# Moving the decay step and the first window's scores ahead of the value, gate and beta projections, adding waits on weights kept in DRAM, and giving one PSUM eviction to VectorE

## What is computed

```python
q, k, v, gate = (xn @ W.T for W in (Wq, Wk, Wv, Wg))        # xn = layernorm(x)
beta  = sigmoid(xn @ Wb.T)
alpha = exp(-exp(A_log) * softplus(xn @ Wa.T + dt_bias))     # one per head and step
q = q / |q| / sqrt(64);  k = k / |k|
for t in steps:                                              # 16 heads, 64x64 state S
    S = S * alpha[t]
    S = S + k[t] (v[t] - k[t] S) * beta[t]
    y[t] = q[t] S
ctx = rmsnorm(y) * silu(gate)
x = x + layernorm(ctx @ Wo.T + bo)
x = x + layernorm(fp6(layernorm(x)) @ fp6(weight).T + bias)
```

## Time and profile before

| | us |
|---|---|
| timed runs, median of 2 | 6981.89 |
| the profiled execution, its own time | 6975.83 |
| span of its slowest core (core 3) | 6974.3 |
| spans of all cores | 6940.6 to 6974.3 |
| mean granted TensorE clock of the cores | 0.587 to 0.589 of 2.4 GHz |

### The profile page before, as it was taken

The page is one execution under the profiler, slowest core; times in us unless marked ns, Lnnn a source line. Parts: engine busy times, 40 slices in busy tenths (PEclk is TensorE's granted clock), DMA queues, the critical chain, the costliest instruction groups (busy, mean ns, idle before and its releaser), DMA issues.

```text
span 6974.3 us, 73066 instructions; the slowest of 8 cores (6940.6 to 6974.3 us)
## 1 busy us (share of the span) xinstructions
PE 2689.2 (39%) x22136; PEld 1582.8 (23%) x22136; DVE 2770.8 (40%) x6430; ACT 1059.7 (15%) x2275; POOL 679.5 (10%) x1048
## 2 busy tenths in 40 slices
PE   2214144444424334544423424445431515444441
PEld 1101022322301122323311113223210103233320
DVE  2341144444462135444453114444455014444446
ACT  2111111111111111111011211111111211111111
POOL 1100110111000111111000111011000011011000
PEclk9999555555557655555556755555555855555555
DMA  5412021212102121212101112112201212121210
GB/s 88 76 36 63 8 43 34 43 35 39 32 18 70 21 37 32 46 31 42 40 14 53 42 26 45 33 31 47 41 21 36 58 14 46 31 38 40 44 32 21
DMA packets 426947, 269.76 MB, mean 39 GB/s; under 512 B 235380, under 2 KB 413942, under 8 KB 426566
## 3 DMA queue, kind: packets, MB, share of 16 engines
q1 hardware_dynamic: 382790, 212.59, 13.8%
q0 software_dynamic: 43776, 52.49, 5.0%
HBM read 245.93 MB, written 27.44 MB: 39 GB/s over the span
## 4 chain that ended last, share of the span: by engine, by line
DVE 32%; DMA 26%; PE 19%; issue 14%; ACT 6%; DVEq 2%; POOL 0%; SPq 0%; ACTq 0%; POOLq 0%
DMA wrep<-wd 13%; DVE ptm L882 8%; DVE u L886 7%; PE ppr L551 3%; DVE rr L625 3%; PE ptr L891 2%; PE psu L904 2%; DMA wdst<-sc 2%; PE pys L917 2%; DVEq L1202 2%; DVE rr L943 2%; PE pys L845 1%; PE ptr L617 1%; ACT ut L896 1%; DVE st L488 1%
## 5 line engine op out<-in xcount | busy, mean ns | idle before, releaser
L891 PE MATMUL ptr<-idf,u 128*16 128x128 f32 x1024 | 259.1, 407 | 1441.2 <-DVE u L886 1336.8
L808 DVE TENSOR_TENSOR wrep<-wrep,bb 128x2048 f32<-128x2048 f32 x128 | 293.4, 2293 | 1082.7 <-DMA wrep<-wd 1082.7
L882 DVE TENSOR_TENSOR ptm<-wrep,u 128x120 f32<-128x120 f32 (+14 forms) x1920 | 515.1, 268 | 193.7 <-DVE u L886 8.0
L886 DVE TENSOR_TENSOR u<-u,ptm 128x120 f32<-128x120 f32 (+14 forms) x1920 | 451.6, 235 | 206.0 <-DVE ptm L882 8.3
L840 PE MATMUL pkv<-kc,s 64*64 64x16 f32 x4096 | 479.6, 265 | 45.2 <-DVE kc L816 45.2
L840 PEld LDWEIGHTS pkv<-kc,s 64*64 64x64 f32 x4096 | 454.3, 220 | 74.0 <-issue 69.9
L845 PE MATMUL pys<-qc,s 64*64 64x16 f32 x4096 | 460.6, 264 | 21.4 <-ACT ys L924 21.4
L891 PEld LDWEIGHTS ptr<-idf,u 128*16 128x16 f32 x1024 | 100.4, 112 | 1587.9 <-issue 1548.2
L845 PEld LDWEIGHTS pys<-qc,s 64*64 64x64 f32 x4096 | 450.6, 222 | 30.2 <-issue 30.2
L551 PE MATMUL ppr<-lt,wrhs 128*128 128x512 bf16 x1280 | 332.7, 407 | 220.9 <-DMA wrhs<-wtk 30.5
L910 DVE TENSOR_TENSOR s<-s,psu 128x512 f32<-128x512 f32 x128 | 88.1, 688 | 752.2 <-PE psu L904 752.2
(11 more groups left out here) (208 smaller groups left out, 4099.0 us busy)
## 6 DMA issues: line engine op xcount, KB each, us to landing
wrep<-wd SPq DMA_DIRECT2D x256, 512.0 KB, 5.2
sx<-x SPq DMA_DIRECT2D x4, 2048.0 KB, 8.6
ao<-pd SPq DMA_DIRECT2D x32, 256.0 KB, 5.7
out<-sx SPq DMA_DIRECT2D x4, 2048.0 KB, 6.6
wld<-Wf SPq DMA_DIRECT2D x8, 512.0 KB, 5.5
wrhs<-wtq POOLq DMA_DIRECT2D x16, 256.0 KB, 3.8
wrhs<-wtq SPq DMA_DIRECT2D x16, 256.0 KB, 3.1
wrhs<-wtk SPq DMA_DIRECT2D x16, 256.0 KB, 3.1
```

The source lines that it names most:

```text
L808: VE(lambda e, wv=wv, bb3=bb3: e.tensor_tensor(wv, wv, bb3, ALU.mult), [f"wrep{cp}", "bb"], [f"wrep{cp}"], tag="wrepscale")
L882: VE(lambda e, wsl=wsl, ub=ub, ptv=ptv: e.tensor_tensor(ptv, wsl, ub, ALU.mult), ["u", f"wrep{cp}"], ["ptm"], tag="slv_p")
L886: VE(lambda e, usl=usl, ptv=ptv: e.tensor_tensor(usl, usl, ptv, ALU.add), ["u", "ptm"], ["u"], tag="slv_u")
L891: TE(lambda e, hp=hp, hpi=hpi: e.transpose(p_tr[0:16, hpi * 128:(hpi + 1) * 128], s_u[:, hp * C:(hp + 1) * C], s_idf[:]), ["u", "idf", "ptr"],
```

## The change

It has four parts.

- **Weight keys.** Every store of a transposed weight now writes a key of its DRAM tensor ("dwq" to "dwb", "dwo", "dwf", "dwa"), and every load of it reads that key.
- **Decay step first.** In `proj_mm_part` the decay step stands before the five projections.
- **Hook.** After the k projection, `norms_window(sb, 0)` and `scores_and_masks(sb, 0)` are called, and not any more after the whole of `proj_mm_part`. `wrep_load(sb*4, 0)` stays behind it.
- **Eviction.** The second round of the u transposes in each chunk is evicted by VectorE.

```diff
@@ prep_weight (the same in the Wo and Wf rounds, with "dwo" and "dwf")
-                dma("sync", dst, src, ["wtt" + "AB"[hb]], [], tag="wstore")
+                dma("sync", dst, src, ["wtt" + "AB"[hb]], ["dw" + tagn],
+                    tag="wstore")
@@ emit_preamble
         dma("sync", d_wat.rearrange("(fb f) h -> f fb h", f=128),
-            s_wtt[:, 0:128].rearrange("f (fb h) -> f fb h", h=16), ["wttA"], ["wttA"])
-        proj_mm_part(0)
+            s_wtt[:, 0:128].rearrange("f (fb h) -> f fb h", h=16), ["wttA"],
+            ["wttA", "dwa"])
+        proj_mm_part(0, hook=lambda: (norms_window(0, 0),
+                                      scores_and_masks(0, 0)))
@@ proj_mm_part
-    def proj_mm_part(sb):
-        projs = [("q", s_qb, AF.Identity), ("k", s_kb, AF.Identity),
...
+    def proj_mm_part(sb, hook=None):
         src = d_wat.rearrange("(fb f) h -> f fb h", f=128)
         dma("sync", s_wrhs[:, 0:128].rearrange("f (fb h) -> f fb h", h=16), src,
-            ["ws0"], ["ws0"])
+            ["ws0", "dwa"], ["ws0"])
...
+        projs = [("q", s_qb, AF.Identity), ("k", s_kb, AF.Identity),
+                 ("v", s_vb, AF.Identity), ("g", s_gb, AF.Silu),
+                 ("b", s_bb, AF.Sigmoid)]
+        for m, dstt, act in projs:
+            for oc in range(8):
...
+                dma("sync" if par == 0 else "gpsimd",
+                    wsl.rearrange("f (fb o) -> f fb o", o=128), src,
+                    skeys + ["dw" + m], skeys, tag="wstream")
...
+            if m == "k" and hook is not None:
+                hook()
@@ proj_superblock
-        proj_mm_part(sb)
+        proj_mm_part(sb, hook=lambda: (norms_window(sb, 0),
+                                       scores_and_masks(sb, 0)))
@@ chunk_steps
-            SE(lambda e, rnd=rnd: e.copy(
-                s_ut[0:16, rnd * 512:(rnd + 1) * 512], p_tr[0:16, 0:512]),
-               ["ptrw"], ["ptr", "ut"])
+            if rnd == 0:
+                SE(lambda e, rnd=rnd: e.copy(
+                    s_ut[0:16, rnd * 512:(rnd + 1) * 512], p_tr[0:16, 0:512]),
+                   ["ptrw"], ["ptr", "ut"])
+            else:
+                VE(lambda e, rnd=rnd: e.tensor_copy(
+                    s_ut[0:16, rnd * 512:(rnd + 1) * 512], p_tr[0:16, 0:512]),
+                   ["ptrw"], ["ptr", "ut"])
@@ attn_out_batch (the same in ffn_superblock with "dwf")
-                [f"ws{cc}"], [f"ws{cc}"], tag="wostream")
+                [f"ws{cc}", "dwo"], [f"ws{cc}"], tag="wostream")
@@ the window loop
             if wi == 0:
-                norms_window(sb, 0)
-                scores_and_masks(sb, 0)
                 wrep_load(sb * 4, 0)
```

More of the change, by code:

```diff
@@ L431, in prep_weight_alt_iter @@
                 "f (fb o) -> f fb o", o=128)
-            dma("sync", dst, srcs, ["tb" + "AB"[hb]], [], tag="wstore")
+            dma("sync", dst, srcs, ["tb" + "AB"[hb]], ["dwo"], tag="wstore")
     def prep_weight_quant_iter(d_src, d_dst, ob):
@@ L459, in prep_weight_quant_iter @@
                 "f (fb o) -> f fb o", o=128)
-            dma("sync", dst, srcs, ["wtt" + "AB"[hb]], [], tag="wstore")
+            dma("sync", dst, srcs, ["wtt" + "AB"[hb]], ["dwf"], tag="wstore")
     def emit_preamble():
@@ L602, in proj_mm_part @@
                ["pscw"], ["psc", "ppt"])
+        projs = [("q", s_qb, AF.Identity), ("k", s_kb, AF.Identity),
[3 more added lines that the diff above has]
+            for oc in range(8):
+                par = oc % 2
+                wsl = s_wrhs[:, par * 1024:(par + 1) * 1024]
+                src = d_wt[m].rearrange("(fb f) o -> f fb o", f=128)[
+                    :, :, oc * 128:(oc + 1) * 128]
+                skeys = [f"ws{par * 2}", f"ws{par * 2 + 1}"]
+                dma("sync" if par == 0 else "gpsimd",
+                    wsl.rearrange("f (fb o) -> f fb o", o=128), src,
+                    skeys + ["dw" + m], skeys, tag="wstream")
+                for fb in range(8):
+                    sk = f"ws{par * 2 + fb // 4}"
+                    TE(lambda e, fb=fb, wsl=wsl: e.matmul(
+                        p_pr[:], wsl[:, fb * 128:(fb + 1) * 128],
+                        s_lt[:, fb * SBT:(fb + 1) * SBT],
+                        start=(fb == 0), stop=(fb == 7)),
+                       [sk, "lt", "ppr"] if fb == 0 else [sk, "lt"],
+                       ["pprw"] if fb == 7 else [])
+                SE(lambda e, dstt=dstt, oc=oc, act=act: e.activation(
+                    out=dstt[:, oc * SBT:(oc + 1) * SBT], in_=p_pr[:], func=act),
+                   ["pprw"], ["ppr", m + "b"])
+            if m == "k" and hook is not None:
+                hook()
     def win_slice(tile, wi, p0=0, p1=128):
@@ L993, in attn_out_batch @@
                         d_wto[cc * 128:(cc + 1) * 128, oh * 512:(oh + 1) * 512],
-                        [f"ws{par2}"], [f"ws{par2}"], tag="wostream")
+                        [f"ws{par2}", "dwo"], [f"ws{par2}"], tag="wostream")
                 for wi in range(4):
@@ L1017, in ffn_superblock @@
                 d_wtf[fb * 128:(fb + 1) * 128, 0:512],
-                [f"ws{fb}"], [f"ws{fb}"], tag="wfstream")
+                [f"ws{fb}", "dwf"], [f"ws{fb}"], tag="wfstream")
         for wi in range(4):
```

2 lines of the change are left out of this document (1 added, 1 removed).

## The result

| | before | after |
|---|---|---|
| median of the timed runs, us | 6981.71 (6 runs, 6979.05 to 6984.73) | 7054.16 (7 runs, 7046.60 to 7057.03) |
| ratio after/before, 95% interval | | 1.0102 (1.0090 to 1.0115) |
| spans of the cores, profiled execution | 6940.6 to 6974.3 | 7012.6 to 7061.9 |

A forecast was written before the change was run, and what follows sets the result against it. The prediction took queue order, not any full engine, as the bound (no chain line above 13%). Its terms 36 + 2 + 4 + 8 = +50 on 6975.8 gave 7026 us, 8-in-10 range 6975 to 7095.

The forecast's parts named there:

- chain of stores: Preamble, five bf16 weights: each store waits for the previous landing, 3.0 us; 6.1 us a round, +36 us (0 to +59).
- Wa read after its store: `d_wat` is read directly after it is written: one landing of 2.0 us, once, +2 us.
- Wo and Wf loads, semaphore turn: Last Wo and Wf blocks on POOL wait for the load just issued: 0 (at most 16 a superblock, under 0.5 us).
- decay step and hook: Superblock reorder moves the DMA row without covering it: start +2.6, restart +6.2, before first chunk -7.8; +4 us in four.
- eviction: VectorE copy in each chunk takes 685 ns against ScalarE's 576; counted in 68 of 128 chunks, +8 us (0 to +14).
- My own sign of being wrong: Among the profile signs listed as "wrong": a landing below 2.6 us in the chained stores.
- b7 to scaling: Before the first chunk: scaling follows b7 by 6.9 us, against 14.7 from "qkb" to scaling today; -7.8 us a superblock.
- the restart: v, g and b resume after "qkb": load 4.0 us, v0's slow matmuls +1.7, v1's wait +0.5; +6.2 us a superblock.
- Stores wholly hidden: Rival: preamble stores land in 2.6 us or less once chained and cost nothing; 6990 us, chance 0.27.
- Hook overlaps: Rival: 24 projection blocks run under the POOL DMA row, 81 us a superblock, 324 in four; 6702 us, chance 0.03.
- Longest landing: Rival: chained preamble stores take 4.3 us to land, 8.7 us a round, +139; 7129 us, chance 0.05.
- Reorder gains: Rival: superblock reorder gains 24 us instead of costing 4, both "wrep" loads fully hidden; 6998 us, chance 0.1.

The follow-up runs named there:

- Run 4: Kernel after with all its keys, but weight keys left out of the waits when a DMA takes over a semaphore: 7037.57 us, 1.0064.
- run 6: Kernel before plus weight keys, kept out of semaphore takeover; loads wait for all stores of their weight, stores not for one another: 6986.55 us, 1.0004.
- run 5: Kernel before plus weight keys, one key for all stores of a weight, kept out of semaphore takeover: 6991.41 us, 1.0013.
- run 3: Kernel after without the weight keys except "dwa" and with evictions on ScalarE, leaving the reorder alone: 7007.38 us, 1.0020.
- run 1: Kernel before with the weight keys alone, order and evictions unchanged: 7038.88 us, 1.0069.
- run 2: Kernel before with only the second round of u transposes evicted by VectorE: 7007.53 us, 1.0026.
- run 7: Kernel before with both rounds of u transposes evicted by VectorE: 7028.01 us, 1.0058.
- Run 10: Against before: decay step first, hook split, v/g/b loaded by SP, "qkb" later, unchained weight keys, semaphore takeover waiting only for the previous DMA: 6603.20 us, 0.9448.
- plain turns: Kernel before, but a DMA taking over a semaphore waits only for its previous DMA, not that DMA's keys' readers: 6955.61 us, 0.9949.

## Why the prediction was right and where it was wrong

The sign, the size class and the mechanism of the reorder were right. That the sum came near is luck: a term that was some 30 us too large and one of about that size that was missing nearly cancelled.

| term, us | forecast | measured |
|---|---|---|
| chain of stores | +36 (0 to 59) | +5 to +9 in the time, +12 in the cores' mean stage |
| Wa read after its store | +2 | not told apart |
| Wo and Wf loads, semaphore turn | 0 (bound: 16 x 0.5 a superblock) | +27 to +39 |
| decay step and hook | +4 (-24 to +48) | +14 |
| eviction | +8 (0 to 14) | +14 to +18 |
| sum | +50 | +72 |

- **Semaphore turn: the step that failed.** "Each is used three blocks later (4 matmuls each), so I put 0." Two things are wrong in it. The distance of three blocks is no cover: in before the load issued at 3555.84 is used at 3558.30, 2.5 us later, and TensorE already waits 0.41 us for it, so each load is issued about one landing ahead of its use and most of any further wait is exposed (3.9 us from two held loads). And I priced that wait at under 0.5 us, with rows at hand that put the landing of a streamed load at 3.0 to 3.8 us; it was 2.93. The POOL loads come 3.5 us apart (3600.41 and 3603.88) where they came 0.86 us apart. I also had the wait too narrow: "the load just issued" is only one of the loads of that key, and the first of the pair was held 2.5 us by SP's. Run 4 shows the cost (28 us in one stage), run 6 that the keys without it are free.
- **Chain of stores: right mechanism, the landing mis-sized.** Forecast was 3.0 us a landing and 6.1 us a round; measured are medians from 2.3 to 3.4 us by weight and 5.64 us a round on core 3, the stores being the bound only in some weights. Of the two rates that I had weighed, both occur. The 0.06 us behind a landing, for which I gave no row, is what before shows between a "wrep" load's landing (2489.05) and the issue of the next (2489.11). My own sign of being wrong, a landing below 2.6 us in the chained stores, came true: the median is 2.3 or 2.4 us in Wk, Wg and Wb. The Trainium skill (DMA: Bandwidth & Descriptors, Latency and other measured facts) has the fixed cost fall with a lighter load on HBM. Wg's 2.3 us would fit that and Wv's 3.4 would not. No run here shows the load on HBM; this core itself moved more in Wg's stretch (107 GB/s from 203.5 to 243.5 us) than in Wv's (83 GB/s from 152 to 203.5), so its own traffic does not explain the difference, and why the landing differs stays open. The slowest core's time moved less than the stage does: 9 us in run 5 against 16 us on core 3 of after. Whether that is because the longest stage falls on another core than the longest rest, no run separates.
- **Decay step and hook: the overlap right, the clock mis-sized.** In the second superblock of after, core 3: start 14.6 us (2208.77 to 2223.39) against 14.5 forecast; norms to "qkb" 156.2 against 157; b7 to scaling 6.0 against 6.9. Two things failed. The first is the restart, "v0's matmuls are slow again, +1.7": three blocks were slow and not one (+5.0). "qkb" to v0 took 5.8 us and not 4.0, since v0's load, beside the "qkb" load, took 5.1 us to land; v1's load waited the "qkb" load out, as forecast. v0 to b7's end is 83.6 us against 79.7 before (2231.39 to 2311.09), where g2 and g3 had been slow instead. That makes 5.8+3.9 = 9.7 where I had 6.2. The second the sum put at nothing: q0 to k7's end takes 59.3 us against 54.3, because six of these 16 blocks run at 3.57 us where two took 3.5 or more before; less one gap between blocks that falls away, +4.1. The superblock's sum is then 2.7+4.1-0.7+9.7-8.7 = +7, +28 in four; in the cores' mean stage A shows +21, and the time of run 3 +14. So the cost of the reorder is about that of a lower clock in the same matmuls: 30 us more busy time on core 3, 28 in the mean of the cores (325 to 353). How much of that hides behind waits for loads no run separates, and both figures scatter: in runs 1, 2, 5 and 6, whose order is that of before, stage A took 1413 to 1416 us where before took 1407, and these matmuls 329 to 335 us.
- **Eviction: right price, wrong count.** 679 ns against 685 forecast. The 68 chunks (139 us at 2.02 are 69) came from L891's share of the chain, but the chain names one of several waits that end together (my reading; no view shows the others); runs 2 and 7 (18 and 41 us, one round and two) say that nearly every chunk pays. From the Trainium skill's cycle table (VectorE: DVE Perf Modes, the section on the TRN2 errata) the estimates were 570 ns for ScalarE and 658 for VectorE. The traces have 575, within 1%, and 679, 3% more.
- **Rivals.** Stores wholly hidden: not so, but nearer than my forecast for this term. Hook overlaps: not in this change, for the reason given, loads held in the queue. Run 10, in which v's loads pass the row of DMAs, has the overlap, and its gain, 352 us without that of the plain turns, is near the 324 us I had worked out; but it also splits the hook, loads v, g and b by SP alone and moves the "qkb" load, and no run tells which of these it needs. Longest landing: no; on the worst core the stage grew by 22 us. Reorder gains: no.

## What to carry to other kernels

When a change adds dependency keys, price not only the data waits but also every rule that looks at the same records: here the rule for reusing semaphores turned a harmless read-after-write key into a landing between neighbouring loads, and in the kernel before it cost 35 us, 28 of which stood in the view of SP's waits. Before calling a prefetch distance a cover, look at whether its user already waits; where it does, most of a new wait is paid. And moving work ahead of a row of chained DMAs gains nothing while its loads stand in the same queue: first take the false waits out of the row (374 us here), or let the loads go by (387 us); both figures have the plain turns' 35 in them. And where a reorder leaves an engine idle, price the lower clock in all that runs behind the gap, and not in one block.

## What the runs showed of the hardware

- **A 128 KB store to DRAM lands in 2.0 to 4.2 us in the same chained stream**, with medians of 2.3 us (Wg) and 3.4 us (Wv) on one core and stages of 208 to 231.5 us on eight. In the kernel before, unchained, the medians of the five weights were 3.0 to 3.3 us.
- **After a pause TensorE kept the lower clock for one to three blocks.** On core 3 there are two matmuls in 60 us, granted 0.50, then 24 matmuls, each eight in 3.57 us, still at 0.50, then 0.96 and 1.89 us. In the 24 superblocks of the six cores of after whose records are complete, v0 took over 3 us in 24, v1 in 16 and v2 in 10, in before none of the three in any: 2.1 slow blocks and 3.5 us a restart in the mean, 5.0 at most, and 1.7 forecast.
- **The lower clock also comes without such a pause**: k1 to k3 of after, 3.57 us each, stand behind 3.49 us without work, and g2 and g3 of before behind no wait above 2.12 us.
- **Small DMAs on POOL overlap well.** Chained by one key, the row of 40 took 110 us, some 2.5 us each and the masks; unchained, eight are issued in 4.5 us (0.56 us each), and the row takes 36 us.
- **What stays open.** The eviction cost 18 us by its ratio where the waits of one chunk give 15; the interval (10 to 26 us) covers both. In run 10 stage A is 395 us shorter in the cores' mean, and what stands behind it 11 us longer. Of the 99 us a superblock, v, g and b, which now run beside the DMAs, took 79.7 in before; where the other 19 come from was not traced.
